# Layer 1 of a four-layer kernel with one weight product for scores, and the ternary test of layer 4's weights on ScalarE

## The chip, the cores and the metric

The kernel runs on one core of a Trainium2 chip. The metric is the device time of one execution in microseconds. The kernel before took 1845.1 us, the median of three runs (1843.9 to 1847.02).

## The reference

Four layers in a row, each `x = x + layernorm(layer(layernorm(x)))`, on x of 4 batches x 1024 tokens x 256 features in float32:

- Layer 1, attention with one head: `q = x Wq`, `k = x Wk`, `v = x Wv`, causal scores `q k^T / 16`, softmax, times v.
- Layer 2: `sqrt((x cos(theta + theta_noise))^2 + (x sin(phi + phi_noise))^2)`, two 256x256 products.
- Layer 3, causal attention with 16 heads of 16 features, and a product with `w_o`.
- Layer 4, a feed-forward net with ternary weights (-1, 0 or 1) and a scale per output: two products 256 to 1024 (SiLU of one times the other), two products 1024 to 1024 with GELU, one back to 256.

## The kernel before

The five engines each get a list of units in a common order, made by `order_first` to `order_fourth`; semaphores join them, and between layers all five meet at a barrier. Products are of split numbers: every operand is a high part (rounded to TensorE's fast float32 type) and a low part (the rest), and `mm3` (L567) makes three products of them: high x high, high x low, low x high. The high part is copied by ScalarE from PSUM, then VectorE subtracts it for the low part (`low`, L1179).

**Layer 1.** For each batch, x is normalised half a batch at a time (`stats1`, `apply1`), turned by TensorE (`tr1`) and split into `xT1`. `qk1(b, h, m, c)` projects a half batch of 512 tokens to queries (m = 0) or keys (m = 1), 128 output features at a time: 6 products of 512 columns. `val1(b, t)` projects two token tiles to values: 12 products of 256 columns. Then come eight tiles of 128 queries. Tile i: `scores1` (6 or 12 products, up to 512 columns each, over the tokens up to the diagonal), VectorE's row maximum (`mx`), ScalarE's exponential (`exps1`), TensorE's transposes of the probabilities (`turn1`), their split on ScalarE and VectorE (`pT_hi`, `pT_lo`), and `weigh1`, the product with the values. The list goes: scores of tile i, turn of tile i-1, exponential of i, then some side work (`side[i]`: the next batch's `tr1`, `qk1`, `val1`, `stats1`, `apply1`), then `weigh1` of tile i-1. Batch 3 has no next batch to project. `xT1` has one buffer; queries, keys and values have two.

Each of the 32 tiles also has one slot for something else. The first nine compute cos and sin for layer 2 (`trig`, `waves`). The later 23 test layer 4's weights: layer 4 has a fast form that is exact only if its weights survive rounding to the fast type, so the kernel reads every weight piece (`PIECES`, 48 of 128 rows x up to 512 columns), rounds it on ScalarE (`rround`, L928) and counts on VectorE where the rounded piece differs (`rcompare`, L1309, which also sums into `changed`). After a comparison SyncE issues the next load into the same buffer (`rload`, L1712). The other 25 pieces are tested in layer 2. `verdict` sums `changed`, and the flag picks the form of layer 4.

**Layer 2.** Eight groups n of four token tiles: `tr2` and `trlo2` turn and split, `tile2` is 6 products of 512 columns, ScalarE squares (`sq`), VectorE adds the squares (`power2`, `pw`, L1349), after the fourth ScalarE takes the root (`root2`, L949). The result is normalised (`ostats2` on VectorE, `stat_out`; `oapply2` on ScalarE, `y` at L968), GpSimd adds it to x (`add2`, L1595). VectorE also normalises group n+2 (`stats2`, `apply2`, `xn` at L1176). VectorE's order within a group: output statistics, a comparison, squares, input statistics, low half, comparison, squares, low half, comparison, squares, four `xn`, comparison, squares.

Of the kernel before, what the change touches and what calls it, by code (L numbers as in the profile page):

```python
# [8 lines left out]
HID = 1024  # L9
# [18 lines left out]
i32 = mybir.dt.int32  # L28
RSQRT_GUESS = float(0x5F3759DF)
# [27 lines left out]
def plain(ap):  # L57

    return ap.bitcast(f32)
# [44 lines left out]

def order_first():

    out, outs, late, todo = [], [], [], []
# [10 lines left out]
    first = NT - TRIG_STEPS  # L118
    rnd = list(range(first))
    loads = list(range(first))  # L120
    for b in range(B):
        side = [[] for _ in range(ST)]
        if b + 1 < B:
            n = b + 1
            p = project(n)
            side = [[("tr1", n, 0, 0), ("tr1", n, 0, 1), ("stats1", n, 1), p[0]], [p[1], ("apply1", n, 1), p[2]],
                    [p[3], ("tr1", n, 1, 0), ("tr1", n, 1, 1)], [p[4], p[5]], [p[6], p[7]], [p[8], p[9]], [p[10]], [p[11]]]
# [6 lines left out]
        for i in range(ST):  # L134
# [29 lines left out]
    out += [("rcompare", n_) for n_ in late]  # L164
# [5 lines left out]
PIECES = [(name, c, o, min(PIECE, cols)) for name, chunks, cols in  # L170
          (("w1", KC, HID), ("w2", KC, HID), ("h1", HC, HID), ("h2", HC, HID), ("w3", HC, D))
          for c in range(chunks) for o in range(0, cols, PIECE)]
FIRST = NT - TRIG_STEPS


def order_second():

    out, outs, late, loads, todo = [], [], [], list(range(FIRST, len(PIECES))), list(range(FIRST, len(PIECES)))
    out += [("rload", loads.pop(0)) for _ in range(4)]

    def settle():
        for u in late:
            out.append(u)
            if u[0] == "rcompare" and loads:
                out.append(("rload", loads.pop(0)))
# [8 lines left out]

    def rnd():
        if todo:
            n = todo.pop(0)
            out.append(("rround", n))
            late.append(("rcompare", n))
# [5 lines left out]
    for n in range(2 * B):  # L205
        for t in range(HALF):
# [13 lines left out]
            rnd()  # L220
    settle()
    out += outs + [("add2", 2 * B - 1)]
    while todo:
        rnd()
        settle()
# [105 lines left out]
def sandwich(nc, x_in, wq0, wk0, wv0, theta, phi, theta_n, phi_n, wqkvT, woT, w1T, w2T, h1T, h2T,  # L331
             w3T, s1, s2, sh1, sh2, s3, out):
    ctx = ExitStack()
    with ctx:
# [10 lines left out]
        hands_back = {"tr1": "dve", "qk1": "dve", "val1": "dve", "turn1": "dve", "weigh1": "act",  # L345
# [114 lines left out]
        with ExitStack() as ph:  # L460
            y1 = sb(ph, "y1", [P, 2, HALF, D])
            flat_y = y1[:, :, :, :].rearrange("p h t d -> p (h t d)")
            xT1 = [sb(ph, f"xT0_{k}", [P, KC, S], f32r) for k in ("hi", "lo")]
            qT = [[sb(ph, f"qT{i}_{k}", [P, KC, S], f32r) for k in ("hi", "lo")] for i in range(2)]
            kT = [[sb(ph, f"kT{i}_{k}", [P, KC, S], f32r) for k in ("hi", "lo")] for i in range(2)]
            v1 = [[sb(ph, f"v{i}_{k}", [P, ST, D], f32r) for k in ("hi", "lo")] for i in range(2)]
            raw1 = sb(ph, "raw", [P, 2, PIECE])
            raw_hi1 = sb(ph, "raw_hi", [P, 2, PIECE], f32r)
# [4 lines left out]
        spare1 = raw1[:, :, :].rearrange("p k (t d) -> p (k t) d", d=D)  # L473
        raw_w0 = [flat_y[:, n * KC * D:(n + 1) * KC * D].rearrange("p (c n) -> p c n", c=KC) for n in range(3)]
        angles = [raw1[:, 0, :], raw1[:, 1, :]]
        noise, turns = plain(raw_hi1[:, 0, :]), plain(raw_hi1[:, 1, :])

        with ExitStack() as ph:
# [5 lines left out]
            raw2 = sb(ph, "raw2", [P, 4, PIECE])  # L484
            raw_hi2 = sb(ph, "raw_hi2", [P, 4, PIECE], f32r)
# [78 lines left out]
        def tensor(e):  # L564
# [24 lines left out]
            def qk1(b, h, m, c):  # L589
                u = ("qk1", b, h, m, c)  # L590
                w.wait_ge(*done("dve", "weights1"))
                w.wait_ge(*back(ring1, u))
# [3 lines left out]
                    [((w0[m][0][:, k, c * P:(c + 1) * P], w0[m][1][:, k, c * P:(c + 1) * P]),  # L596
                      (xT1[0][:, k, cols], xT1[1][:, k, cols])) for k in range(KC)]).then_inc(*mark("pe", "qk1"))

            def val1(b, t):
                u = ("val1", b, t)  # L600
                bank = ring1.bank[u]
                w.wait_ge(*back(ring1, u))
                w.wait_ge(*done("dve", "tr1", b, 1, 1))
                for n in range(2):
                    tok = slice((t + n) * P, (t + n + 1) * P)
                    m = mm3(psum[:, bank, n * D:(n + 1) * D], [((xT1[0][:, k, tok], xT1[1][:, k, tok]),
# [35 lines left out]
            perform("first", {"tr1": tr1, "qk1": qk1, "val1": val1, "scores1": scores1, "turn1": turn1, "weigh1": weigh1,  # L642
# [212 lines left out]
        def scalar(e):  # L855
# [8 lines left out]
            def tr1(b, h, c):  # L864
                w.wait_ge(*done("pe", "tr1", b, h, c))
                if b:
                    w.wait_ge(*done("pe", "val1", b - 1, ST - 2))
                e.activation(xT1[0][:, c, h * BANK:(h + 1) * BANK], psum[:, ring1.bank["tr1", b, h, c], :],
                             ACT.Copy).then_inc(*mark("act", "tr1"))

            def qk1(b, h, m, c):
                w.wait_ge(*done("pe", "qk1", b, h, m, c))
                if b > 1:
                    w.wait_ge(*done("pe", "weigh1", b - 2, ST - 1))
                e.activation((qT, kT)[m][b % 2][0][:, c, h * BANK:(h + 1) * BANK], psum[:, ring1.bank["qk1", b, h, m, c], :],
# [48 lines left out]
            def rround(n, raw, hi, first, bufs, tag):  # L924
                k, cols = (n - first) % bufs, PIECES[n][-1]
                w.wait_ge(sem(f"rload{tag} {k}"), 16 * ((n - first) // bufs + 1))
                w.wait_ge(*nth("dve", "rcompare", n - bufs if n - first >= bufs else -1))
                e.activation(hi[:, k, 0:cols], raw[:, k, 0:cols], ACT.Copy).then_inc(*mark("act", "rround"))  # L928

            perform("first", {"weights1": weights1, "tr1": tr1, "qk1": qk1, "val1": val1, "exps1": exps1, "turn1": turn1,  # L930
                              "weigh1": weigh1, "waves": waves, "rround": lambda n: rround(n, raw1, raw_hi1, 0, 2, 1),
# [32 lines left out]
            def oapply2(n):  # L964
                rstd, term = moments["out"][3:]
                w.wait_ge(*done("dve", "ostats2", n))
                for t in range(HALF):
# [5 lines left out]
                               "rround": lambda n: rround(n, raw2, raw_hi2, FIRST, 4, 2),  # L973
# [164 lines left out]
        def vector(e):  # L1138
# [84 lines left out]
            def tr1(b, h, c):  # L1223
                w.wait_ge(*done("act", "tr1", b, h, c))
                cols = slice(h * BANK, (h + 1) * BANK)
                low("tr1", xT1[1][:, c, cols], psum[:, ring1.bank["tr1", b, h, c], :], xT1[0][:, c, cols])

            def qk1(b, h, m, c):
                w.wait_ge(*done("act", "qk1", b, h, m, c))
                cols, T = slice(h * BANK, (h + 1) * BANK), (qT, kT)[m][b % 2]  # L1230
                low("qk1", T[1][:, c, cols], psum[:, ring1.bank["qk1", b, h, m, c], :], T[0][:, c, cols])
# [73 lines left out]
            def rcompare(n, raw, hi, first, bufs):  # L1305
                k, cols = (n - first) % bufs, PIECES[n][-1]
# [51 lines left out]
            def verdict():  # L1358
                w.wait_ge(*done("dve", "rcompare", len(PIECES) - 1))
# [5 lines left out]
                               "power2": power2, "ostats2": ostats2, "rcompare": lambda n: rcompare(n, raw2, raw_hi2, FIRST, 4),  # L1365
# [320 lines left out]
        def sync(e):  # L1686
# [19 lines left out]
            def rload(n, raw, first, bufs, tag):  # L1706
                name, c, o, cols = PIECES[n]
                if tag == 1:
                    w.wait_ge(*done("dve", "waves"))
                if n - first >= bufs:  # L1710
                    w.wait_ge(*done("dve", "rcompare", n - bufs))
                e.dma_start(raw[:, (n - first) % bufs, 0:cols],  # L1712
                            weights[name][c * P:(c + 1) * P, o:o + cols]).then_inc(sem(f"rload{tag} {(n - first) % bufs}"), 16)

            def xloads(n):
                for k in range(n, 2 * B):
# [3 lines left out]
                              "rload": lambda n: rload(n, raw1, 0, 2, 1), "end": lambda: barrier(e, w, "first")})  # L1720
# [117 lines left out]
```

## Time and profile before

| | us |
|---|---|
| median of three runs | 1845.1 |
| the profiled execution | 1851.76 |
| its span | 1850.0 |
| TensorE busy | 1601.2 (87%) |
| VectorE busy | 1010.3 (55%) |
| ScalarE busy | 831.3 (45%) |
| GpSimd busy | 425.9 (23%) |
| mean granted TensorE clock | 0.894 |

PE is TensorE, PEld its weight loads, DVE VectorE, ACT ScalarE, POOL GpSimd, SP SyncE; SPq is SyncE's DMA issue. Layer 1 fills the first 278.3 us of the span and layer 2 the next 120.8. A row of a timeline gives start, duration, engine, line, operation, output and input, count, and in brackets how long the engine sat idle and what ended that. TensorE's products overlap: the distance of two starts, not the duration, tells what one costs.

### The profile page before, as it was taken

To read this page: it belongs to the slowest core of one execution; us is meant where nothing else is said; L and a number is where in the kernel's file an instruction comes from. 1 tells how busy PE (TensorE), PEld (TensorE's weight loads), DVE (VectorE), ACT (ScalarE), POOL (GpSimd) and SP (SyncE) were. 2 spreads that over 40 slices of the span, in tenths; PEclk is the share of its full clock that TensorE was granted. 3 is DMA by queue.
4 is the path that set the end of the run, shared out by engine and by line. 5 is a ranking of instruction groups with operands and counts; after the bars stand their busy time and mean duration, and the time that the engine had idled before them with its cause. 6 is when DMAs were issued, how large, how long until landed. Compare 5 with 4: busy or idle time off the path is not lost.

```text
span 1850.0 us, 24362 instructions
## 1 busy us (share of the span) xinstructions
PE 1601.2 (87%) x8658; PEld 1130.1 (61%) x8658; DVE 1010.3 (55%) x2889; ACT 831.3 (45%) x1686; POOL 425.9 (23%) x927
## 2 busy tenths in 40 slices
PE   6988856625799999998999995599999999999996
PEld 5877754524345445444545333488888888888885
DVE  5867547843766777767686832223334343333432
ACT  3454425631246565655565662234334353433432
POOL 2222221140233256235414323100101001010101
PEclk9999987867569799979998877699999999999998
DMA  3011102225603540741263100900000000000000
GB/s 120 12 35 35 46 17 89 88 80 74 86 1 47 82 71 13 96 59 44 42 87 59 36 2 23 289 12 0 23 1 23 1 24 1 23 23 1 12 1 23
DMA packets 52930, 83.34 MB, mean 45 GB/s; under 512 B 6784, under 2 KB 41216, under 8 KB 49920
## 3 DMA queue, kind: packets, MB, share of 16 engines
q1 hardware_dynamic: 46512, 68.85, 18.9%
q0 software_dynamic: 5712, 12.06, 2.1%
q10 hardware_dynamic: 576, 0.79, 0.4%
q8 instruction: 70, 1.15, 0.3%
q14 instruction: 60, 0.49, 0.1%
HBM read 43.40 MB, written 12.58 MB: 30 GB/s over the span
## 4 chain that ended last, share of the span: by engine, by line
PE 68%; DVE 16%; ACT 5%; issue 4%; POOL 2%; DMA 2%; SPq 1%; POOLq 1%; ACTq 0%; DVEq 0%
PE psum L831 25%; PE psum L571 13%; PE psum L746 7%; PE psum L805 6%; PE psum L731 6%; PE psum L712 4%; PE psum L844 3%; DVE mxs L1412 3%; PE psum L575 3%; DVE masked L1418 3%; ACT pr L1036 2%; DVE stat_out L1145 1%; DVE stat_in L1145 1%; SPq L1753 1%; DVE raw L1309 1%
## 5 line engine op out<-in xcount | busy, mean ns | idle before, releaser
L831 PE MATMUL psum<-fh_hi,fWh 128*128 128x512 f32 x1024 | 399.0, 390 | 0.0
L831 PE MATMUL psum<-fh_lo,fWh 128*128 128x512 f32 x1024 | 398.4, 389 | 0.0
L1036 ACT ACTIVATE pr<-psum 128x512 f32<-128x512 f32 (+3 forms) x768 | 321.8, 493 | 136.6 <-PE psum L731 131.4
L1181 DVE TENSOR_TENSOR fh_lo<-fraw,fh_hi 128x512 fp32r<-128x512 f32 x192 | 132.9, 692 | 380.0 <-ACT fh_hi L1100 335.3
L1418 DVE CUSTOM_DVE_ANT_0 masked<-psum,later 128x128 bf16<-128x128 f32 (+3 forms) x512 | 220.8, 487 | 96.8 <-PE psum L712 95.3
L731 PE MATMUL psum<-Qs,Ks 50*128 50x512 f32 (+3 forms) x768 | 234.1, 423 | 20.9 <-ACT pr L1036 12.3
L1096 ACT ACTIVATE fraw<-psum,fsch 128x512 f32<-128x512 f32 x128 | 86.5, 676 | 301.6 <-PE psum L831 301.6
L712 PE MATMUL psum<-Ks,Qs 48*128 48x512 f32 (+3 forms) x768 | 181.9, 466 | 40.3 <-DVE mxs L1418 18.0
L831 PEld LDWEIGHTS psum<-fh_lo,fWh 128*128 128x128 f32 x1024 | 192.3, 188 | 39.7
L831 PEld LDWEIGHTS psum<-fh_hi,fWh 128*128 128x128 f32 x1024 | 192.2, 188 | 39.7
L746 PE MATMUL psum<-pr,va 128*32 128x512 f32 (+3 forms) x1536 | 188.1, 566 | 0.0
L731 PEld LDWEIGHTS psum<-Qs,Ks 50*128 50x128 f32 x768 | 120.8, 209 | 107.0 <-ACT pr L1036 69.6
L712 PEld LDWEIGHTS psum<-Ks,Qs 48*128 48x128 f32 x768 | 84.3, 212 | 153.2 <-issue 59.1
L1412 DVE TENSOR_REDUCE mxs<-psum 128x2 f32<-128x1024 f32 x128 | 149.9, 1216 | 38.1 <-PE psum L712 37.9
L1580 POOL TENSOR_TENSOR term_in<-rstd_in 128x4 f32<-128x4 f32 x66 | 14.5, 220 | 518.4 <-DVE rstd_in L1162 515.0
L1649 POOL TENSOR_SCALAR_AFFINE_SELECT pr<-pr 128x512 f32<-128x512 f32 x128 | 81.9, 641 | 130.4 <-ACT pr L1036 130.0
L805 PE MATMUL psum<-fxT_hi,fWw 128*128 128x512 f32 x256 | 101.4, 396 | 10.7 <-DMA fWw<-in_w1T 10.2
L805 PE MATMUL psum<-fxT_lo,fWw 128*128 128x512 f32 x256 | 100.9, 394 | 0.0
L1100 ACT ACTIVATE fh_hi<-fraw 128x512 fp32r<-128x512 f32 x128 | 80.9, 632 | 4.0
L1580 POOL TENSOR_TENSOR term_out<-rstd_out 128x4 f32<-128x4 f32 x78 | 17.4, 223 | 274.0 <-DVE rstd_out L1162 269.9
L1595 POOL TENSOR_TENSOR x<-x,y 128x1024 f32<-128x1024 f32 x16 | 40.5, 2529 | 132.0 <-ACT y L968 97.8
L571 PE MATMUL psum<-v_hi,pT_hi 128*128 128x256 f32 x144 | 46.3, 321 | 25.5 <-DVE pT_lo L1181 25.3
(228 smaller groups left out, 2807.6 us busy)
## 6 DMA issues: line engine op xcount, KB each, us to landing
Qs<-q_hi SPq DMA_DIRECT2D x60, 128.0 KB, 5.4
Ks<-k_hi SPq DMA_DIRECT2D x60, 128.0 KB, 5.0
xr<-x_stream SPq DMA_DIRECT2D x9, 512.0 KB, 4.4
x<-in_x SPq DMA_DIRECT2D x8, 512.0 KB, 8.0
raw<-in_h1T SPq DMA_DIRECT2D x16, 256.0 KB, 2.6
raw<-in_h2T SPq DMA_DIRECT2D x16, 256.0 KB, 2.8
x_stream<-x SPq DMA_DIRECT2D x8, 512.0 KB, 3.2
shared_xn<-x_stream SPq DMA_DIRECT2D x8, 512.0 KB, 5.6
```

What stands on the lines that cost most here:

```text
L571: m = e.matmul(o, l, r, start=start and n == 0, stop=stop and n == len(ops) - 1)
L712: e.matmul(psum[:, pairs3.bank[u] + side, 0:width], Qs[g % NST][r, pair, i * P:(i + 1) * P], Ks[g % NST][r, pair, k0:k0 + width], start=Tr ...
L731: e.matmul(psum[:, ring3.bank[u], 0:width], Ks[g % NST][r, pair, j * P:(j + 1) * P], Qs[g % NST][r, pair, q0:q0 + width], start=True, stop ...
L746: m = e.matmul(psum[32 * ct:32 * ct + VB, 7, BANK - width:BANK], va[b % 2][:, j, head * VW:head * VW + VB], pr[:, 2 * (s % 3) + pair, side ...
L805: m = e.matmul(psum[:, bank, :], f.W[name][:, c, cols], xT[:, n % 2, c, :], start=(c, k) == (0, 0), stop=(c, k) == last)
L831: m = e.matmul(psum[:, ring4.bank[u], :], f.W[name][:, c, oc * P:(oc + 1) * P], h[:, c, :], start=(c, k) == (0, 0), stop=(c, k) == last)
L1036: e.activation(pr[:, 2 * (s % 3) + pair, side, 0:width], psum[:, ring3.bank["st3", s, pair, side], 0:width], ACT.Exp, scale=SC1).then_inc( ...
L1096: e.activation(f.raw[:, k, :], psum[:, bank, :], ACT.Gelu, scale=f.sc[("h1", "h2")[layer]][:, oc:oc + 1]).then_inc(*mark("act", "dense4"))
L1181: return e.tensor_tensor(dst, src, plain(hi), ALU.subtract).then_inc(*mark("dve", kind))
L1412: m = e.tensor_reduce(mxs[:, g % 2, k0 // BANK, :, pair, i], psum[:, bank:bank + 2, 0:width], AX.X, ALU.max)
L1418: m = e.tensor_tensor_reduce(masked[:, 2 * pair + side, 0:width], psum[:, bank + side, 0:width], later[:, BANK - width:], 1.0, LEAST, ALU. ...
L1649: e.affine_select(out=blocks, in_=blocks, compare_op=ALU.is_ge, fill=0.0, base=0, pattern=[[0, 2], [0, 2], [1, P]], channel_multiplier=-1) ...
```

## The change

In layer 1 the queries' and keys' weights are multiplied with each other: `fold1` makes `Wq Wk^T` (2 units of 6 products of 256 columns), split into `wm`. One projection `qk1(b, h, c)` with `wm` takes the place of queries and keys, and the scores are formed against `xT1`, which now has two buffers. So 4 units of `qk1` per batch go, with their copies and subtractions. `Wq` and `Wk` are laid out transposed. The units stand in another order: in batch 0 a value unit first, then the fold, the other values, then the queries; for the later batches one query unit in each of tiles 0, 1, 4 and 5, and one value unit in each of tiles 3, 5, 6 and 7.

The weight test reads pieces of 128 x 1024 numbers (22 in all, each 512 KB, two buffers). `weighed` is one ScalarE activation over the low 16 bits of every number, taken as unsigned integers, that sums them into `changed`; rounding to the fast type can only matter where they aren't zero. It overwrites the piece. The comparison on VectorE is gone. All 22 stand in layer 1, one in each tile's slot from tile 1 of batch 1 on; layer 2 has none.

```diff
+PIECES = [(name, c, n) for name, chunks, n in (("w1", KC, 1), ("w2", KC, 1), ("h1", HC, 1), ("h2", HC, 1), ("w3", HC, HC // 2))
+          for c in range(0, chunks, n)]
...
     def project(b):
-        return ([("qk1", b, half, m, c) for half in range(2) for m in range(2) for c in range(KC)]
-                + [("val1", b, t) for t in range(0, ST, 2)])
+        return ([("val1", b, t) for t in range(0, ST, 2)] + [("qk1", b, half, c) for half in range(2) for c in range(KC)])
-    out += project(0) + [("apply1", 1, 0)]
+    vals = project(0)[:ST // 2]
+    out += vals[:1] + [("fold1", 0), ("fold1", 1)] + vals[1:] + project(0)[ST // 2:] + [("apply1", 1, 0)]
...
-            side = [[("tr1", n, 0, 0), ("tr1", n, 0, 1), ("stats1", n, 1), p[0]], [p[1], ("apply1", n, 1), p[2]],
-                    [p[3], ("tr1", n, 1, 0), ("tr1", n, 1, 1)], [p[4], p[5]], [p[6], p[7]], [p[8], p[9]], [p[10]], [p[11]]]
+            side = [[("tr1", n, 0, 0), ("tr1", n, 0, 1), ("stats1", n, 1), p[4]], [p[5], ("apply1", n, 1)],
+                    [("tr1", n, 1, 0), ("tr1", n, 1, 1)], [p[0]], [p[6]], [p[1], p[7]], [p[2]], [p[3]]]
...
-                for n_ in late:
-                    out.append(("rcompare", n_))
+                if rnd:
+                    out.append(("weighed", rnd.pop(0)))
                     if loads:
                         out.append(("rload", loads.pop(0)))
-                late = [rnd.pop(0)]
-                out.append(("rround", late[0]))
...
+            def fold1(c):
+                u = ("fold1", c)
                 w.wait_ge(*done("dve", "weights1"))
+                w.wait_ge(*back(ring1, u))
+                mm3(psum[:, ring1.bank[u], 0:D],
+                    [((w0[0][0][:, k, c * P:(c + 1) * P], w0[0][1][:, k, c * P:(c + 1) * P]), (w0[1][0][:, k, :], w0[1][1][:, k, :]))
+                     for k in range(KC)]).then_inc(*mark("pe", "fold1"))
+            def qk1(b, h, c):
+                u, X = ("qk1", b, h, c), xT1[b % 2]
+                w.wait_ge(*done("dve", "fold1", 1))
...
             def scores1(b, i):
-                n, Q, K = b * ST + i, qT[b % 2], kT[b % 2]
+                n, Q, K = b * ST + i, qT[b % 2], xT1[b % 2]
...
+                w.wait_ge(*done("dve", "qk1", b, 1, 1))
...
+            def weighed(n):
+                piece = pieces1[n % 2]
+                w.wait_ge(sem(f"rload {n % 2}"), 16 * (n // 2 + 1))
+                e.activation(piece, piece.bitcast(u16).rearrange("p (n k) -> p n k", k=2)[:, :, 0], ACT.Copy,
+                             accum_out=changed[:, n:n + 1]).then_inc(*mark("act", "weighed"))
...
-            def rcompare(n, raw, hi, first, bufs):
-                k, cols = (n - first) % bufs, PIECES[n][-1]
-                w.wait_ge(*done("act", "rround", n))
-                r = raw[:, k, 0:cols]
-                e.scalar_tensor_tensor(r, r, 1.0, plain(hi[:, k, 0:cols]), ALU.mult, ALU.not_equal,
-                                       accum_out=changed[:, n:n + 1]).then_inc(*mark("dve", "rcompare"))
...
+            def rload(n):
+                name, c, chunks = PIECES[n]
+                w.wait_ge(*done("dve", "waves"))
+                if n > 1:
+                    w.wait_ge(*done("act", "weighed", n - 2))
+                e.dma_start(pieces1[n % 2].rearrange("p (c n) -> p c n", c=chunks),
+                            rows(weights[name])[:, c:c + chunks, :]).then_inc(sem(f"rload {n % 2}"), 16)
...
-        "x": a["L0_attn_x"], "wq0": a["L0_attn_Wq"], "wk0": a["L0_attn_Wk"], "wv0": a["L0_attn_Wv"],
+        "x": a["L0_attn_x"], "wq0": a["L0_attn_Wq"].T, "wk0": a["L0_attn_Wk"].T, "wv0": a["L0_attn_Wv"],
```

## Rows read from the trace of the kernel before

**Rows 1.** By stretch: its length; PE, PEld, DVE, ACT, POOL busy; clock; DMA share

```profile
0.00:38.70 38.70, 22.90 (x118) 19.86 (x118) 22.39 (x63) 12.52 (x20) 9.77 (x48) 1.00 0.45 143
38.70:208.40 169.70, 154.56 (x982) 134.63 (x982) 123.89 (x354) 81.67 (x174) 41.10 (x125) 0.97 0.09 28
208.40:278.30 69.90, 42.85 (x249) 37.48 (x246) 34.32 (x117) 21.60 (x48) 19.14 (x51) 0.82 0.09 28
278.30:399.10 120.80, 69.56 (x258) 52.43 (x258) 90.08 (x292) 65.71 (x130) 19.53 (x8) 0.75 0.27 85
399.10:1850.00 1450.90, 1311.37 (x7056) 885.72 (x7056) 739.61 (x2065) 649.78 (x1315) 336.38 (x695) 0.90 0.23 42
```

**Rows 2.** Chain of waits in layer 1 (start, duration, what)

```profile
62.92 6.31 PE psum L571 x36
...
168.28 0.60 DVE kT_lo L1181
168.88 0.61 DVE raw L1309 x2
```

**Rows 3.** Timeline of the opening, TensorE's products and one VectorE pair

```profile
17.95 0.78 PE L571 MATMUL psum<-xT_hi,w_hi 128*128 128x512 f32 x1
...
19.37 0.63 PE L571 MATMUL psum<-xT_hi,w_hi 128*128 128x512 f32 x1
19.58 1.28 DVE L1181 TENSOR_TENSOR xT_lo<-psum,xT_hi 128x512 fp32r<-128x512 f32 x2
19.80 0.63 PE L571 MATMUL psum<-xT_lo,w_hi 128*128 128x512 f32 x1
...
24.88 0.39 PE L571 MATMUL psum<-xT_hi,w_lo 128*128 128x512 f32 x1
25.11 0.39 PE L571 MATMUL psum<-xT_hi,w_hi 128*128 128x512 f32 x1
...
31.03 0.28 PE L571 MATMUL psum<-w_hi,xT_hi 128*128 128x256 f32 x1
31.15 0.28 PE L571 MATMUL psum<-w_lo,xT_hi 128*128 128x256 f32 x1
```

**Rows 4.** First test of a piece; 512 KB loads; a 1024-column activation

```profile
107.36 10.32 SPq L1712 DMA_DIRECT2D raw<-in_w1T  x3
109.99 0.64 ACT L928 ACTIVATE raw_hi<-raw 128x512 fp32r<-128x512 f32 x1
...
xr<-x_stream SPq DMA_DIRECT2D x9, 512.0 KB, 4.4
x<-in_x SPq DMA_DIRECT2D x8, 512.0 KB, 8.0
...
L949 ACT ACTIVATE y<-pw 128x1024 f32<-128x1024 f32 x8 | 8.5, 1058 | 22.8 <-DVE pw L1349 22.8
```

**Rows 5.** Chain of waits in layer 2, the start of two groups

```profile
311.03 1.41 DVE stat_out L1145 x4
...
325.23 1.08 DVE stat_out L1145 x3
```

**Rows 6.** Timeline of layer 2 about GpSimd's add, in two groups

```profile
317.70 2.07 ACT L968 ACTIVATE y<-y,term_out,rstd_out 128x256 f32<-128x256 f32 x4
319.74 3.43 DVE L1176 TENSOR_SCALAR xn<-x,mv_in,rstd_in 128x256 f32<-128x256 f32 x4
319.84 2.53 POOL L1595 TENSOR_TENSOR x<-x,y 128x1024 f32<-128x1024 f32 x1 [11.69 <-ACT y L968]
323.31 1.09 PE L575 MATMUL psum<-ident,xn 128*128 128x128 f32 x4 [1.40 <-DVE xn L1176]
323.70 0.41 DVE L1349 TENSOR_TENSOR pw<-sq 128x256 f32<-128x256 f32 x1
...
372.68 2.39 POOL L1595 TENSOR_TENSOR x<-x,y 128x1024 f32<-128x1024 f32 x1 [8.73 <-ACT y L968]
373.12 2.24 DVE L1349 TENSOR_TENSOR pw<-sq 128x256 f32<-128x256 f32 x1 [1.58 <-ACT sq L943]
```

More of the change, by code:

```diff
@@ L28 @@
 i32 = mybir.dt.int32
+u16 = mybir.dt.uint16
 RSQRT_GUESS = float(0x5F3759DF)
@@ L102 @@
     ("val", "val1 val3")) for kind in kinds.split()}
+PIECES = [(name, c, n) for name, chunks, n in (("w1", KC, 1), ("w2", KC, 1), ("h1", HC, 1), ("h2", HC, 1), ("w3", HC, HC // 2))
+          for c in range(0, chunks, n)]
 def order_first():
-    out, outs, late, todo = [], [], [], []
+    out, outs = [], []
     pre = [[("stats1", b, h) for h in range(2)] for b in range(B)]
@@ L112, in project @@
     def project(b):
-        return ([("qk1", b, half, m, c) for half in range(2) for m in range(2) for c in range(KC)]
-                + [("val1", b, t) for t in range(0, ST, 2)])
-    out += project(0) + [("apply1", 1, 0)]
+        return ([("val1", b, t) for t in range(0, ST, 2)] + [("qk1", b, half, c) for half in range(2) for c in range(KC)])
+    vals = project(0)[:ST // 2]
+    out += vals[:1] + [("fold1", 0), ("fold1", 1)] + vals[1:] + project(0)[ST // 2:] + [("apply1", 1, 0)]
     trig = [u for n in range(2) for u in (("trigload", n), *[("trig", n, k) for k in range(3)])] + [("waves",)]
-    first = NT - TRIG_STEPS
-    rnd = list(range(first))
-    loads = list(range(first))
+    rnd = list(range(len(PIECES)))
+    loads = list(range(len(PIECES)))
     for b in range(B):
@@ L167, in order_first @@
     return out + [u for u in outs if u] + [("end",)]
[L170 to L173, printed above, removed]
 def order_second():
-    out, outs, late, loads, todo = [], [], [], list(range(FIRST, len(PIECES))), list(range(FIRST, len(PIECES)))
-    out += [("rload", loads.pop(0)) for _ in range(4)]
+    out, outs, late = [], [], []
     def settle():
@@ L193, in tr @@
         late.append(("trlo2", n, c))
[L195 to L199, printed above, removed]
     tr(0, 0)
@@ L595, in qk1 @@
                 mm3(psum[:, ring1.bank[u], :],
-                    [((w0[m][0][:, k, c * P:(c + 1) * P], w0[m][1][:, k, c * P:(c + 1) * P]),
-                      (xT1[0][:, k, cols], xT1[1][:, k, cols])) for k in range(KC)]).then_inc(*mark("pe", "qk1"))
+                    [((wm[0][:, k, c * P:(c + 1) * P], wm[1][:, k, c * P:(c + 1) * P]),
+                      (X[0][:, k, cols], X[1][:, k, cols])) for k in range(KC)]).then_inc(*mark("pe", "qk1"))
             def val1(b, t):
-                u = ("val1", b, t)
+                u, X = ("val1", b, t), xT1[b % 2]
                 bank = ring1.bank[u]
+                w.wait_ge(*done("dve", "weights1"))
                 w.wait_ge(*back(ring1, u))
@@ L1225, in tr1, with fold1, qk1 @@
                 cols = slice(h * BANK, (h + 1) * BANK)
[L1226 to L1231, printed above, removed]
+                low("tr1", xT1[b % 2][1][:, c, cols], psum[:, ring1.bank["tr1", b, h, c], :], xT1[b % 2][0][:, c, cols])
+            def fold1(c):
+                w.wait_ge(*done("act", "fold1", c))
+                low("fold1", wm[1][:, c, :], psum[:, ring1.bank["fold1", c], 0:D], wm[0][:, c, :])
+            def qk1(b, h, c):
+                w.wait_ge(*done("act", "qk1", b, h, c))
+                cols, T = slice(h * BANK, (h + 1) * BANK), qT[b % 2]
+                low("qk1", T[1][:, c, cols], psum[:, ring1.bank["qk1", b, h, c], :], T[0][:, c, cols])
             def val1(b, t):
@@ L1358, in verdict @@
             def verdict():
-                w.wait_ge(*done("dve", "rcompare", len(PIECES) - 1))
+                w.wait_ge(*done("act", "weighed", len(PIECES) - 1))
                 e.tensor_reduce(cnt[:, :], changed[:, :], AX.X, ALU.add).then_inc(*mark("dve", "verdict"))
@@ L1719, in sync @@
             perform("first", {"weights1": weights1, "xload": xloads, "trigload": trigload,
-                              "rload": lambda n: rload(n, raw1, 0, 2, 1), "end": lambda: barrier(e, w, "first")})
+                              "rload": rload, "end": lambda: barrier(e, w, "first")})
             def add2(n):
```

74 lines of the change are left out of this document (25 added, 49 removed).

## The prediction

> **What bounds the kernel now.** The table by stretch comes first [rows 1]. Layer 1 takes the first 278.3 us: an opening of 38.7 (first halves loaded and normalised, batch 0 projected), batches 0 to 2 in 169.7, batch 3 in 69.9. Layer 2 ends at 399.1; layers 3 and 4 take the other 1450.9, and the diff leaves their code alone. In batches 0 to 2 TensorE is busy 154.6 of 169.7 us at a granted clock of 0.97. In batch 3, which has no next batch to project, it is busy 42.9 of 69.9. In layer 2 VectorE is busy 90.1 of 120.8 and TensorE 69.6.
>
> Next comes the chain of waits [rows 2]. In the tiles where a projection stands beside large score products it is TensorE alone: 36 products in 6.31 us. In the small tiles it is VectorE, and there both things that the change takes away stand in it: the low half of a key (0.60) and the comparison of a weight piece (0.61), each just ahead of the row maximum that lets the next exponential start. In layer 2 the chain is VectorE nearly throughout: one group of four tiles, from one start of `stat_out` to the next, takes 14.20 us [rows 5] and holds four comparisons.
>
> The profiled execution took 1851.76 us for its span of 1850.0. The median of the three timed runs is 1845.1, 6.7 less. I work out differences in the trace and take them from the median.
>
> **Layer 1, opening.** Before: 48 products of 512 columns and 48 of 256. At full clock they start 0.23 and 0.12 us apart, in the first 3.4 us 0.43 apart [rows 3]: 8 x 0.43 + 40 x 0.232 + 48 x 0.12 = 18.5. After: 24 of 512 and, with the fold's 12, 60 of 256. With 3.4 us at the low level for the first 16, this is 3.4 + 44 x 0.12 + 24 x 0.232 = 14.3, so 4.2 less. But the first unit is now a value projection, and that waits for the last low half of x^T, which VectorE ends at 19.58 + 1.28 = 20.86; the first query projection started at 17.95 [rows 3]. That gives 2.9 back: -1.3. The fold's eviction (two copies, two subtractions of 256 columns) lies beside 36 value products of 0.12, 4.3 us: nothing. Without that cover it would cost about 2.
>
> **Batches 0 to 2.** Each loses 24 products of 512 columns (24 x 0.232 = 5.6 us of TensorE), four copies on ScalarE and four subtractions on VectorE. Not all of it can be had, since the new lists leave tile 2 with transposes alone and tile 3 with one value unit. Once the next scores are done, the way to the weighted sum is maximum, reciprocal, low half of the turned probabilities: about 1.3 us at tile 2, 1.6 at tile 3, 1.9 at tile 4 (0.35 for the small instructions, the rest grows with the tile). I went tile by tile and took at each the later of TensorE's list and VectorE's list.
> - Batch 2. Tile 1: the comparison ahead of the maximum goes (0.6), then a key's low half and another comparison (1.2) [rows 2]. Tile 2: again one of each, 1.3. Tile 4: six products fewer, 1.4. Tiles 5 to 7 keep their length, because a query unit (6 x 0.232) takes the place of a value unit (12 x 0.12). Together 4.5.
> - Batch 0. VectorE computes the angles there and there are no comparisons: 0.6 at each of tiles 1 and 2, 1.4 at tile 4. Together 2.6.
> - Batch 1. 0.6 at tile 1, 1.3 at tile 2, 1.4 at tile 4, 0.5 at tile 7, less the wait below: 3.8 - 1.3 = 2.5.
>
> **The test on ScalarE.** A 128x1024 activation took 1.06 us [rows 4]; with reading the accumulator I take 1.25, against 0.64 for the old rounding of 512 columns. No row shows one that reads every other 16-bit word; from below it is 1.06, from above twice that. It stands behind the eviction of the weighted sum and ahead of the copy of the turned probabilities. From tile 3 on the next scores (1.4 us and more) cover it, and at tile 1 VectorE's statistics do. At tile 0 of batches 2 and 3 the scores are 128 columns wide and nothing does: 0.5 each, so batch 1 comes to -2.0 and batch 2 to -4.0. At 2.1 us each the test would stand out in about half of the 22 tiles by 0.8, some 9 us: that end is kept for the range.
> The test also has a new wait: its piece is 512 KB. The first load is issued at 107.36 as before, and the old test began at 109.99 [rows 4]. A 512 KB load landed in 4.4 us, which is 111.8. ScalarE stands still until then, and behind it wait the copy of the turned probabilities, the next exponential and the evictions: 1.8 us late, plus the longer test, less what TensorE has to do meanwhile; I take 1.3, once. Later pieces are loaded two tiles ahead (9 us in the small tiles), so at 4.4 they are there.
>
> **Batch 3.** Only comparisons go. Two stood ahead of a maximum, one ahead of the last low half (0.6 each) [rows 2]; the others ran under TensorE: -1.9. Layer 1 in all: 1.3 + 2.6 + 2.0 + 4.0 + 1.9 = 11.8.
>
> **Layer 2.** 25 comparisons go (17 of 512 columns at 0.61 [rows 2], 8 of 256 at 0.34, an estimate from it: 13.1 us of VectorE), with 25 copies on ScalarE and their loads. What is late next? After four additions of squares the group needs GpSimd's add, and while this runs VectorE stands: of four normalisations started at 319.74 two passed, and the four ended only 0.8 after the add of 319.84 to 322.37; an addition of squares, 0.41 by itself, took 2.24 under the add of 372.68 [rows 6]. Laid out anew from the start of `stat_out`, with each instruction's duration as in this group: statistics 2.4, squares 0.34, input statistics to 5.1, two low halves and two squares to 7.0. ScalarE, after the input's root, a copy and a square, ends its four `y` (2.07) at 7.7 and the add runs from 7.75 to 10.2. The normalisations mostly pass ahead of it, but the last squares end 0.3 to 0.7 after the add; with root (1.06) the next group starts at 11.6 to 12.1. Mean 11.85: 2.35 less in each of three groups, 1.5 and 1.3 in the two with three and four pieces of 256 columns (each piece 0.27 shorter from the start), 1.1 in the first, where TensorE is late next: 11.0. TensorE at its low level needs 24 x 0.43 [rows 3] + 2 x 1.09 [rows 6] = 12.5 for a group; its clock was 0.75 here [rows 1], so I take 0.8 off: -10.2. The bounds are -7, if always at the low level, and -13.1, all that is removed.
> The Trainium skill has the reason for this limit (GPSIMD Engine Reference, Specifications): GpSimd shares its SBUF interfaces with VectorE and contends with VectorE's instructions that have two SBUF inputs. The trace agrees by that 2.24 against 0.41 [rows 6]. Were it not so, the group would be near 10 us and layer 2 some 19 shorter.
>
> Sum: 11.8 + 10.2 = 22.0, and 1845.1 - 22.0 gives **1823**.
>
> **Rivals.**
> A. All of it is had: the tiles stay bound by TensorE (72 x 0.232 = 16.7), opening 1.3, comparisons in layer 1 2.9, layer 2 13.1: 34.0, 1811. For it: 91% busy in batches 0 to 2. Against it: kT_lo and the comparison stand in the chain, so TensorE already waited there, and the add holds layer 2.
> B. ScalarE holds the tiles: the test is nearer 2 us or its loads land late (of eight loads of this size issued together in the opening the median landed in 8.0 [rows 4]), 0.6 in each of 22 tiles: 22 - 13 = 9, 1836. Against it: ScalarE was busy 81.7 of 169.7 [rows 1].
> C. **Slower.** TensorE's clock in batches 0 to 2. With gaps at tiles 2 and 3 it may be granted less than 0.97. Its work at full clock is 154.6 x 0.97 - 16.7 = 133.3, beside 15 us of idle: at 0.75, the clock of layer 2, 133.3 / 0.75 + 15 = 192.7, 23 more than now. Opening, batch 3 and a layer 2 at its low bound give 10 back: 1858. It decides below 0.81 (133.3 / 0.81 + 15 = 179.6, 10 more). For it: batch 3 had just 0.82 at 61% busy, and layers 3 and 4 had 0.90 at 90% [rows 1]. Against it: the new share is about 46 of 54 us, near the present one, and gaps stay under 3 us.
> D. The low halves don't come out as zero and layer 4 takes its other branch: hundreds of us. Weights of -1, 0 and 1 have empty low halves: 0.01.
>
> **Chances.** Forecast 0.62, A 0.13, B 0.18, C 0.06, D 0.01. The range 1810 to 1836 reaches from A to B. A measurement of this kernel tells 0.2%, 3.7 us, from no change. Faster 0.91 (forecast, A, nearly all of B), same 0.03, slower 0.06.
>
> **What would show it.** Opening: first product of batch 0 near 20.9, first scores near 37.4. Batches 0 to 2 in about 161 us with TensorE still at 0.95 or more and idle 16 to 19; one ScalarE wait of about 2 us for `raw` at the first test and none later; tests of 1.06 to 1.1 us. Layer 2's groups at 11.6 to 12.4, with the squares held to the add's end. Layers 3 and 4 within 2 us of 1451. The forecast is wrong if the tests make ScalarE the releaser of the small tiles, if the clock falls, or if the groups of layer 2 stay above 13.

## The result, and the profile after

The changed kernel took 1822.8 us (median of four runs, 1816.4 to 1824.1) against 1844.5 for the kernel before (four runs, 1839.7 to 1847.0): a ratio of 0.988, 95% interval 0.985 to 0.991, or 21.7 us less. The forecast was 1823.0. Its profiled execution took 1824.12 us for a span of 1822.4, at a clock of 0.898. Executions over 1.5% longer than the fastest of their kernel, all at a low clock, are left out of the medians and ratios below.

The table by stretch, first of the kernel before with batches 0 to 3 apart, then of the changed kernel. The cuts stand where a batch's first scores are complete (the small product with `tri` behind them), and "first scores at" means that mark throughout. Columns as in [rows 1]; the clock is the mean of the stretch, and a "low stretch" is one of some 4 us in which it falls to 0.50 or near it.

```profile
38.70:91.70 53.00, 48.67 (x307) 42.32 (x306) 41.44 (x112) 22.43 (x49) 10.89 (x37) 0.97 0.03 11
91.70:150.30 58.60, 52.75 (x339) 46.05 (x338) 43.03 (x128) 31.36 (x66) 16.59 (x50) 0.97 0.11 32
150.30:208.10 57.80, 52.84 (x339) 45.97 (x339) 39.35 (x115) 27.57 (x62) 13.61 (x38) 0.97 0.12 39
208.10:278.30 70.20, 43.15 (x252) 37.78 (x250) 34.39 (x117) 21.90 (x49) 19.14 (x51) 0.82 0.09 29
```

```profile
0.00:38.40 38.40, 19.78 (x106) 17.71 (x106) 20.48 (x61) 10.89 (x18) 9.77 (x48) 1.00 0.44 144
38.40:90.20 51.80, 45.48 (x283) 39.59 (x283) 39.27 (x108) 20.51 (x45) 10.90 (x37) 0.90 0.04 11
90.20:145.60 55.40, 49.00 (x314) 43.77 (x312) 37.47 (x113) 32.77 (x68) 15.21 (x50) 0.91 0.23 76
145.60:197.10 51.50, 45.55 (x315) 40.27 (x315) 31.72 (x93) 29.66 (x66) 11.91 (x38) 1.00 0.25 83
197.10:263.30 66.20, 40.74 (x253) 36.04 (x251) 28.81 (x99) 25.38 (x56) 16.54 (x51) 0.89 0.16 48
263.30:371.00 107.70, 64.61 (x259) 48.40 (x259) 76.94 (x242) 54.33 (x105) 19.26 (x9) 0.80 0.13 44
371.00:1822.40 1451.40, 1310.02 (x7056) 884.16 (x7056) 739.22 (x2065) 650.00 (x1315) 336.53 (x695) 0.90 0.23 42
```

Both layers got shorter: layer 1 from 278.3 to 263.3, layer 2 from 120.8 [rows 1] to 107.7. Together that is 28.1 us, six more than forecast, and six more than the medians differ; layers 3 and 4 stand at 1451.4 against 1450.9. In batches 0 and 1 the clock was 0.90 and 0.91 instead of 0.97, in batch 2 it was 1.00.

In the opening, the first product and two pairs further on (timeline):

```profile
21.12 0.55 PE L550 MATMUL psum<-w_hi,xT_0hi 128*128 128x256 f32 x1 [2.71 <-DVE xT_0lo L1175]
...
25.31 0.41 PE L550 MATMUL psum<-w_lo,w_hi 128*128 128x256 f32 x1
25.52 0.41 PE L550 MATMUL psum<-w_hi,w_lo 128*128 128x256 f32 x1
...
26.32 0.28 PE L550 MATMUL psum<-w_hi,xT_0hi 128*128 128x256 f32 x1
26.44 0.28 PE L550 MATMUL psum<-w_lo,xT_0hi 128*128 128x256 f32 x1
```

The first unit waits for the low half of x^T, as worked out. But a distance of 0.21 from start to start, instead of the 0.12 of [rows 3], lasts to 26.2. That is 5.1 us instead of the 3.4 assumed, although the clock column says 1.00 here. I call this the half rate.

The test, as groups of ScalarE's instructions and its first start:

```profile
L922 ACT ACTIVATE raw<-raw 128x1024 f32<-128x1024 uint16 x22 | 23.1, 1052 | 1.1 <-DMA raw<-in_w1T 1.1
L922 ACT ACTIVATION_READ_ACCUMULATOR raw<-raw 128x1 f32 x22 | 4.2, 192 | 0.0
...
108.77 1.06 ACT L922 ACTIVATE raw<-raw 128x1024 f32<-128x1024 uint16 x1 [1.15 <-DMA raw<-in_w1T]
```

Each takes 1.05 us and 0.19 for the accumulator, the 1.25 assumed. There is one wait for a load, 1.15 us, and none later.

Layer 2 about GpSimd's add (timeline; the second line is the last of the first line's four), and the chain of waits of the same group:

```profile
299.08 3.42 DVE L1170 TENSOR_SCALAR xn<-x,mv_in,rstd_in 128x256 f32<-128x256 f32 x4
300.05 2.45 DVE L1170 TENSOR_SCALAR xn<-x,mv_in,rstd_in 128x256 f32<-128x256 f32 x1
299.89 2.46 POOL L1585 TENSOR_TENSOR x<-x,y 128x1024 f32<-128x1024 f32 x1 [9.30 <-ACT y L963]
302.42 0.41 DVE L1339 TENSOR_TENSOR pw<-sq 128x256 f32<-128x256 f32 x1
```

```profile
292.19 1.41 DVE stat_out L1139 x4
...
299.16 1.20 DVE xn L1170 x4
300.36 2.06 issue
...
303.96 1.08 DVE stat_out L1139 x3
```

The group lasts 303.96 - 292.19 = 11.77 us against the 14.20 of [rows 5]; 11.85 was forecast. The 2.06 of "issue" in the chain is the stall: three normalisations took 0.40 each, the fourth began 0.16 after the add and ended 0.15 after it (299.89 + 2.46 = 302.35), and the last squares, the root and the next group follow. But the same stall stood in the kernel before, where the second of the four was held, begun 0.22 after the add's start at 319.84 and ended 0.15 after its end (timeline):

```profile
320.06 2.46 DVE L1176 TENSOR_SCALAR xn<-x,mv_in,rstd_in 128x256 f32<-128x256 f32 x1
```

There the four took 3.43, here 3.42. So the group lost just its four comparisons, 14.20 - 4 x 0.61 = 11.76, and layer 2 lost the whole 13.1 us that VectorE was spared (busy 90.1 before, 76.9 after). By its length alone the group can't tell the forecast's account from the one by which all that is removed is had; the experiment with the short add, below, shows what the add is worth.

### The profile page after: what moved, and what is told of

It reads as the page before. It is cut to its first block, busy times and chain, and to the rows that moved or that the text cites. A ratio compares the mean times of both kernels' runs of the same rounds, so it can differ in the third digit from the quotient of the medians.

```text
span 1822.4 us, 24003 instructions
## 1 busy us (share of the span) xinstructions
PE 1575.2 (86%) x8574; PEld 1109.9 (61%) x8574; DVE 973.9 (53%) x2779; ACT 823.5 (45%) x1668; POOL 420.1 (23%) x927
## 3 DMA queue, kind: packets, MB, share of 16 engines
q8 instruction: 70, 1.15, 0.3%
## 4 chain that ended last, share of the span: by engine, by line
PE 69%; DVE 15%; ACT 5%; issue 5%; POOL 2%; DMA 2%; SPq 1%; POOLq 1%; ACTq 0%; DVEq 0%
PE psum L821 25%; PE psum L550 13%; PE psum L736 7%; PE psum L795 6%; PE psum L721 6%; PE psum L702 4%; PE psum L834 3%; DVE masked L1408 3%; PE psum L554 3%; DVE mxs L1402 3%; ACT pr L1030 2%; DVE stat_out L1139 1%; DVE stat_in L1139 1%; SPq L1742 1%; DVE mx L1242 1%
## 5 line engine op out<-in xcount | busy, mean ns | idle before, releaser
L702 PE MATMUL psum<-Ks,Qs 48*128 48x512 f32 (+3 forms) x768 | 180.1, 461 | 42.9 <-DVE mxs L1408 20.9
L554 PE MATMUL psum<-ident,shared_xn 128*128 128x128 f32 x128 | 23.8, 335 | 51.9 <-issue 19.2
L550 PE MATMUL psum<-v_hi,pT_hi 128*128 128x256 f32 x144 | 45.5, 316 | 25.8 <-DVE pT_lo L1175 25.7
```

The source lines that it names most:

```text
L550: m = e.matmul(o, l, r, start=start and n == 0, stop=stop and n == len(ops) - 1)
L702: e.matmul(psum[:, pairs3.bank[u] + side, 0:width], Qs[g % NST][r, pair, i * P:(i + 1) * P], Ks[g % NST][r, pair, k0:k0 + width], start=Tr ...
```

## The experiments

Every one has a trace. The ends of layers 1 and 2 repeat in them, while the whole does not: three profiled executions of the changed kernel reached layer 3 at 371.0, 371.3 and 369.5 us and then spent 1451.4, 1471.8 and 1444.4 us in layers 3 and 4. So the stretches carry the verdicts, and the medians stand beside them. The kernel before has one trace, so every gain by stretches counts from that one, and gains under 2 us are inside what the three traces differ by.

**The control.** The same code, run beside the next three.

> The changed kernel unaltered, as control and for a second trace. Theory (the gain is instructions removed, not clock): 20 to 23 us under the kernel before, 1.3 to 4 of it in each of batches 0 to 3, layer 2 at 107.7 us as in the first trace. Rival (part of what the first trace showed is the clock the execution happened to be granted): the clocks of batches 0 and 1 (0.90 and 0.91 in the first trace, 0.97 before) and of the last tile of batch 3 come out otherwise here, the ends of the batches move by 1 to 3 us with them, while the time of the whole stays within 3 us of 1822.8.

Layers 1 and 2 came out as in the first trace within 0.3 us, low stretches included; what differs is the last row:

```profile
90.20:145.70 55.50, 49.10 (x315) 43.88 (x315) 37.49 (x113) 32.88 (x68) 15.29 (x50) 0.91 0.22 76
...
371.30:1843.10 1471.80, 1331.78 (x7056) 894.58 (x7056) 740.51 (x2065) 650.63 (x1315) 337.58 (x695) 0.88 0.22 41
```

The median was 1821.4 (4 runs) against 1847.7 for the kernel before in the same set (13 runs), ratio 0.986 (0.979 to 0.994). The rival's clocks did not move here.

**The fold alone.** The diff's first part with the old test (copy, compare, pieces of 512 columns):

```
 weights' product, value units first, x^T as keys     as changed
-("weighed", n)
+("rround", n), ("rcompare", n)      # 23 pieces in layer 1, 25 in layer 2
```

> Only the first part of the change: folded weights, values first, x^T as keys; the old copy-and-compare test with pieces of 512 columns stays, in layers 1 and 2. Theory: the opening gives 0.3 to 1.3, batches 0 to 2 some 7 to 8 (0.6 to 1.4 at tiles 1, 2 and 4), batch 3 nothing, layer 2 stays at 120.8 with groups of 14.2: 7 to 9 us under the kernel before, near 1836. Rival (the thinner TensorE lists of tiles 2 and 3 leave the comparisons uncovered, or the clock falls): 5 us or less. Rival (TensorE's busy time is what counts): 17 us.

```profile
37.40:90.20 52.80, 46.65 (x282) 40.65 (x281) 39.31 (x108) 20.60 (x45) 10.90 (x37) 0.87 0.04 11
90.20:146.20 56.00, 48.45 (x314) 42.92 (x313) 40.79 (x124) 29.61 (x62) 16.55 (x50) 0.94 0.10 34
146.20:201.00 54.80, 47.38 (x315) 41.51 (x315) 37.02 (x112) 25.68 (x58) 13.60 (x38) 0.97 0.12 41
201.00:271.00 70.00, 42.90 (x252) 37.42 (x250) 34.29 (x117) 21.91 (x49) 19.16 (x51) 0.82 0.09 29
271.00:391.70 120.70, 69.38 (x258) 52.18 (x258) 90.13 (x292) 65.71 (x130) 19.53 (x8) 0.75 0.27 85
```

Layer 3 is reached 7.4 us earlier, inside the 7 to 9 expected: opening 1.3, batches 0.2, 2.6 and 3.0, batch 3 and layer 2 nothing. The batches' 5.8 is under the 7 to 8 expected for them: batch 0 gained just 0.2, at a clock of 0.87 instead of 0.97. The medians say 6.2 less (1841.5, 9 runs), but the ratio's interval, 0.996 (0.992 to 1.001), holds no change too.

**The test alone.** The diff's second part; queries and keys are projected apart as before.

```
-("fold1", c), ("qk1", b, half, c), keys = xT1[b % 2]
+("qk1", b, half, m, c),            keys = kT[b % 2]
```

> Only the second part: the test of the low halves by one activation on ScalarE, 22 pieces of 1024 columns, all in layer 1; queries and keys are projected apart as before. Theory: the comparisons' 0.6 us ahead of the maximum in batches 1 to 3 go (about 4 us), 1.3 to 2 come back in the wait for the first piece and the uncovered tests, and layer 2 gives 10 to 13: 12 to 15 us under the kernel before, near 1831, with layer 2 at 108 to 110. With the fold alone it adds up to the whole, 21.7, within 2. Rival (the ScalarE work in layer 1's tiles costs what VectorE is spared): layer 1 no shorter than 278 and 10 to 11 in all.

```profile
92.30:150.50 58.20, 52.42 (x339) 46.08 (x339) 39.78 (x117) 34.55 (x72) 15.27 (x50) 0.97 0.21 73
150.50:206.90 56.40, 52.40 (x338) 45.99 (x338) 34.11 (x97) 31.46 (x69) 11.92 (x38) 0.97 0.22 76
206.90:273.10 66.20, 40.65 (x251) 36.01 (x250) 28.80 (x99) 25.29 (x55) 16.55 (x51) 0.88 0.14 48
273.10:380.70 107.60, 63.55 (x259) 47.75 (x259) 76.96 (x242) 54.33 (x105) 19.29 (x9) 0.82 0.13 44
```

Layer 3 is reached at 380.7, 18.4 earlier: more than expected, 5.2 of it in layer 1 (the theory had 2 to 3) and 13.2 in layer 2. The medians say 18.0 less (1829.8, 4 runs; ratio 0.989, 0.982 to 0.996). With the fold's 7.4 that makes 25.8 of the whole's 28.1: the parts add up within 2.3.

**The add made short.** `add2` over one of a group's four tiles; three quarters of layer 2's addition to x are left out.

```
-add("add2", x[:, n * HALF:(n + 1) * HALF, :], y2[:, n % 2, :, :], ...)
+add("add2", x[:, n * HALF:n * HALF + 1, :], y2[:, n % 2, 0:1, :], ...)
```

> The changed kernel with GpSimd's addition of layer 2's result made over one of a group's four tiles; three quarters of that addition are left out. Theory (the add holds VectorE, and the group's 11.75 us come from it): the add takes about 0.65 instead of 2.46, the four normalisations 1.4 instead of 3.4, and the group falls to 10 to 10.5; layer 2 from 107.7 to 98 to 101. Rival (what ends the group is TensorE, or the sum of VectorE's own instructions): groups stay within 0.4 of 11.75.

```profile
297.02 1.80 DVE L1170 TENSOR_SCALAR xn<-x,mv_in,rstd_in 128x256 f32<-128x256 f32 x4
297.83 0.83 POOL L1585 TENSOR_TENSOR x<-x,y 128x256 f32<-128x256 f32 x1 [9.30 <-ACT y L963]
```

```profile
290.14 1.41 DVE stat_out L1139 x4
...
298.30 0.43 issue
...
300.28 1.41 DVE stat_out L1139 x4
```

The group fell to 10.14 us, the four normalisations from 3.42 to 1.80, the stall from 2.06 to 0.43, and layer 2 from 107.7 to 94.7, below the range expected. So the add's stall stands in the group in full: 1.63 us less of it is 1.63 us less group, and TensorE didn't hold it back.

**No test.** Its loads and activations are left out, the verdict set to zero; and **the test one tile later**, so that the first piece has landed.

```
-out.append(("weighed", rnd.pop(0)))            # no test; no ("rload", n) either
+if rnd and n > 9: out.append(("weighed", ...)) # later test, instead
```

> The changed kernel without the test of layer 4's weights: its loads and its 22 activations are left out, the verdict is set to zero. Theory: the wait for the first piece (1.15 us) and the tests that stand out at tile 0 of batches 1 to 3 go, the rest was covered: layer 1 shorter by 2 to 3 us, layer 2 as it is. Rival (ScalarE holds the small tiles): 6 us or more. Rival (the loads disturb other transfers or the test costs nothing): within 0.5.

> The changed kernel with every test one tile later, the first load issued where it was. Theory: the piece has landed when ScalarE comes to it, the wait of 1.15 us at the first test goes and no other comes: batch 1 shorter by about 1 us, the last test still inside batch 3. Rival (TensorE, at its low level from 104 to 112 us, was late there anyway): batch 1 the same within 0.3 us.

Batches 1 to 3 without the test, then batches 1 and 3 with it one tile later:

```profile
90.30:145.70 55.40, 49.01 (x314) 43.88 (x313) 37.51 (x113) 26.75 (x55) 15.30 (x50) 0.91 0.00 1
145.70:196.90 51.20, 45.46 (x314) 40.23 (x313) 31.73 (x93) 21.66 (x49) 11.96 (x38) 1.00 0.01 1
196.90:264.00 67.10, 41.83 (x252) 36.41 (x251) 28.91 (x99) 17.40 (x40) 16.62 (x51) 0.86 0.00 1
```

```profile
90.30:145.50 55.20, 48.29 (x314) 43.01 (x314) 37.40 (x113) 31.70 (x65) 15.31 (x50) 0.94 0.20 67
...
198.50:266.90 68.40, 42.22 (x253) 37.53 (x251) 28.80 (x99) 26.27 (x58) 16.62 (x51) 0.85 0.17 54
```

Without 27 us of tests (23.1 + 4.2) batches 1 and 2 together are 0.3 us shorter, batch 3 is 0.9 longer at a lower clock, and layer 1 ends 0.7 later. In layer 1 the test costs nothing that the traces show, its wait for the load included: with only that wait taken away batch 1 was 0.2 shorter. In both traces TensorE was in a low stretch at that tile. Where it was not, in the trace with the short add, the wait was 1.46 us, and from that tile's exponential to the next took 4.2 us, against 3.8 at the same tile of batch 2, where nothing waits: 0.4 at most. The second kernel's layer 1 ended 3.6 later, by its clock as far as the traces tell: the opening was 1.0 shorter, but batch 0 gave back 1.1 (0.87), batch 2 1.5 (0.97 instead of 1.00), batch 3 2.2 (0.85; it also holds one test more). Both theories failed; the rivals held.

**The fold made early.** In the changed kernel TensorE idles from 18.4 to 21.1 and before 13.1. Here the weights are multiplied ahead of the second half's normalisation, and the queries come first again:

```
-("apply1", 0, 0), ("apply1", 0, 1), ...
-out += vals[:1] + [("fold1", 0), ("fold1", 1)] + vals[1:] + <queries>
+("apply1", 0, 0), ("fold1", 0), ("fold1", 1), ("apply1", 0, 1), ...
+out += <queries> + <values>
```

> The whole change, but the product of the two weights is computed before the second half of batch 0 is normalised, and batch 0's query products come ahead of its value products as in the kernel before. Theory: TensorE has the fold done in its idle time before the transposes and starts batch 0's products at about 18 instead of 21.1, on the first half of x^T alone; first scores 2 to 3 us earlier than 38.4, the whole 2 to 3 us under the changed kernel (near 1820). Rival (VectorE, which must make the fold's two low halves first, normalises the second half of the batch later by 1 to 2 us, and TensorE then runs dry after the first half): first scores no more than 1 us earlier, the whole within 1 us.

```profile
11.35 0.55 PE L549 MATMUL psum<-w_hi 128*128 128x256 f32 x1 [11.35 <-DVE w_lo L1213]
...
18.30 0.40 PE L549 MATMUL psum<-xT_0hi,wm_lo 128*128 128x512 f32 x1
18.54 0.39 PE L549 MATMUL psum<-xT_0hi,wm_hi 128*128 128x512 f32 x1
```

Batch 0 starts at 17.76, at 0.23 to 0.31 per product of 512 columns from the first on, and the first scores come at 32.05 instead of 38.42: 6.4 us, twice the expectation. The early products themselves, from 11.35 on, were 0.21 apart. The median was 1815.4 (5 runs) beside the control's 1821.4 (ratio to the kernel before 0.981, 0.975 to 0.987). This expectation hadn't reckoned with the slow first products. To part the two causes:

> The early fold, but with batch 0's value products ahead of its query products as in the changed kernel. The early fold with the queries first had its first scores at 32.05 us against 38.4. Theory: of those 6.4 us, 3.4 are the earlier start on the first half of x^T and fall away here; 3.0 are the fold's 12 products taken out of the stretch and the products at full rate from the first on, since TensorE has multiplied at 11.4 us already, and stay: first product at 21, spaced 0.12 at once, first scores at 35 to 35.5. Rival (the slow rate comes with the first products after any pause): spaced 0.21 for some 3 us again, first scores near 37.5.

```profile
21.03 0.55 PE L549 MATMUL psum<-w_hi,xT_0hi 128*128 128x256 f32 x1 [3.53 <-DVE xT_0lo L1174]
21.38 0.41 PE L549 MATMUL psum<-w_lo,xT_0hi 128*128 128x256 f32 x1
...
22.00:26.00 4.00, 4.00 (x21) 4.00 (x20) 0.69 (x1) 0.60 (x1) 0.80 (x4) 0.50 0.01 2
```

With the values first and 3.5 us of idleness ahead of them the products are 0.21 apart again and the first scores come at 37.05: the rival held. Here the clock column does show it, as 0.50. An early fold by itself gives 0.4 to 1.4 against the changed kernel's 37.5 to 38.4; the other 5.0 (37.05 to 32.05) came from the order, by which batch 0 starts 3.3 us sooner and at full rate. The half rate lasted 5.6 us in this one trace, the longest of all, so up to an us of that split is its chance.

**Where the clock falls.** In the traces with the fold, a low stretch stood in batch 0 near 52 us, behind tile 2, which has transposes alone. So six products went from tile 1 to tile 2, on the changed kernel and on the early fold:

```
-[p[5], ("apply1", n, 1)], [("tr1", n, 1, 0), ("tr1", n, 1, 1)]
+[("apply1", n, 1)], [p[5], ("tr1", n, 1, 0), ("tr1", n, 1, 1)]
```

> The changed kernel with one query product group (six products of 512 columns) moved from tile 1 to tile 2 of each batch, where TensorE had transposes alone. In three traces with the fold TensorE's granted clock fell in batch 0 near 52 us, right behind that thin tile, and in batch 1 near 104; in the kernel before and in the one with the new test alone it did not. Theory (the thin tile 2 brings the fall): the low stretches at 52 and 104 us go, batches 0 and 1 shorter by 1 to 3 us each. Rival (the fall follows the whole share of work, not this tile): a low stretch of the same length stands somewhere in batches 0 and 1, and they are the same within 1 us.

> The early fold (queries first) with the same six products moved from tile 1 to tile 2. If the thin tile brings the fall of the clock: layer 1 ends at 252 to 255 us instead of 256.8, the whole 2 to 5 us under the early fold. If not: within 1 us of 256.8.

```profile
37.80:88.40 50.60, 44.45 (x281) 38.62 (x280) 39.09 (x108) 20.49 (x45) 10.92 (x37) 0.93 0.04 11
88.40:145.90 57.50, 49.30 (x314) 43.82 (x314) 37.30 (x113) 32.86 (x68) 15.35 (x50) 0.91 0.21 74
...
200.30:268.60 68.30, 43.01 (x252) 37.31 (x251) 29.05 (x99) 25.44 (x56) 16.57 (x51) 0.82 0.14 47
```

Batch 0 won 1.2 us and its fall at 52 went, but the one at 104 stayed, batches 1 and 2 became 2.1 and 2.9 longer and layer 1 ended 5.3 later. On the early fold, layer 1 ended at 257.6, between that kernel's own 256.8 and 258.5. The thin tile explains neither the clock nor the time; what does stays open. The two kernels' times, 1819.6 (one run) and 1808.2 (median of 5; ratio 0.979, 0.973 to 0.984), lie with those of the changed kernel and the early fold.

**The early fold beside the changed kernel.**

> The early fold once more, beside the changed kernel on the same chip. Theory: its opening and batches repeat (first scores at 32.1, layer 1 ends at 256.8), and the whole is 6 to 7 us under the changed kernel. Rival (layers 3 and 4 give it back through the clock): the traces repeat, but the whole is less than 3 us under.

> The changed kernel beside the early fold. Theory: first two layers as in the two traces before (layer 2 starts at 263.3 to 263.6, layer 3 at 371.0 to 371.3), 20 to 25 us under the kernel before. Rival (the low stretches of the clock fall elsewhere in each execution): these two marks move by more than 1 us.

Layer 3 was reached at 365.9 and 369.5 (364.4 and 371.0, 371.3 before): 5.4 us apart in the mean. The medians are 1810.9 (5 runs; ratio 0.976, 0.969 to 0.984) and 1817.6 (6 runs; 0.984, 0.978 to 0.990) against 1847.1. So the early fold is the fastest here in both sets, by its traces some 5 us; the intervals of the two ratios overlap. In the third trace of the changed kernel the slow stretches did fall elsewhere: its half rate ended at 24.5 instead of 26.2 (first scores at 37.5), batch 1 had 0.97 and took 53.8 instead of 55.4, and batch 2 had 0.97 and took 53.0 instead of 51.5.

## Why the prediction was right, and where by luck

The direction and the median were right, and most of the mechanisms. The sum, 22.0, is 6 us short of what layers 1 and 2 gave, 28.1 in the first pair of traces; that is as far from the forecast as from rival A's 34.0.

- **Opening**: forecast -1.3, got -0.3. The start (21.12 against 20.9) was right. The half rate was taken as 3.4 us and lasted 5.1; where it ended at 24.0 instead of 26.2 (the fold alone, first scores at 37.4), the 1.3 were there.
- **Batches 0 to 2**: forecast -8.6 at a clock of 0.95 or more, got -10.7 at 0.94; idle time was 158.7 - 140.0 = 18.7, inside the 16 to 19. Batch 0 gave 1.2 instead of 2.6, at 0.90 instead of 0.97. Batch 1 gave 3.2 instead of 2.0, batch 2 6.3 instead of 4.0. The term that failed is **the test's cost in them**: 1.3 for the wait at the first piece and 0.5 at tile 0 of batches 2 and 3 each, 2.3 in all. Taken out altogether, the test gave back 0.3. The wait was there, 1.15 us of the 2 expected, and next to nothing came of it. What else is off goes with the clock as far as the traces tell, and cancels: in the traces where batch 2 had 0.97, as before, it took 52.9 to 53.0, so 1.5 of its 6.3 came with the 1.00, while batch 0, at 0.93, took 50.6 (the shifted list) and 50.7 (values first), near the forecast's 50.4, but also 51.9 (the early fold again).
- **Batch 3**: forecast -1.9, got -4.0. The comparisons' 1.9 is right at an unchanged clock: with the new test and 0.82, this batch took 68.3 (the shifted list) against 70.2. The rest goes with the clock: in the traces the batch took 68.3 at 0.82, 68.4 at 0.85, 67.1 at 0.86, 66.0 to 66.4 at 0.88 and 0.89, 64.8 at 0.91, and with the old test 70.0 to 70.2 at 0.82. Why the clock was mostly higher with the new test isn't shown.
- **Layer 2**: forecast -10.2, got -13.1, the end of its range. The three middle groups gave 7.16 against 7.05 (add to add, 42.34 to 35.18 us), the next two 2.8 as forecast. The first (to its add) gave 2.5 where I had put 1.1, because TensorE should have been late next; the end gave 0.6 where I had nothing; and the 0.8 for the low clock was not due: TensorE kept up at 0.80. What failed is the thought that something would be held back. The add's stall was in the group before and after, at the same length, and moved up with the group, so all that was removed was had. (The recorded reading that two of the four passed ahead of the add at 319.84 is off by one: the second was the held one.) That the add holds VectorE is right: the short add gave 10.14 us a group, where I had written near 10. Yet layer 2 was then 26.1 shorter than before, not 19.
- **Layers 3 and 4**: within 0.5 us of 1450.9 in the trace. By the medians, less layer 3's start and the 1.7 us around the span, they took 1844.5 - 1.7 - 399.1 = 1443.7 before and 1822.8 - 1.7 - 371.0 = 1450.1 after, though their code is the same. That difference hid my shortfall. It is most likely the clock, though the record has none for the four runs before. An estimate from the runs that have one: over 80 executions of six kernels, with the clock of layers 3 and 4 worked out from each run's mean and the traces, their time falls by 11.3 us for each 0.01, with a scatter of 2.1, and at 0.90 lies between 1446.2 and 1449.4 in all. Whether the changed kernel's 0.1 to 1.4 us more there than the kernel before (1447.0) is real stays open.
- **The rivals.** A (all of it is had) was near in layer 2, where its 13.1 came, and wrong in the tiles, where it had 16.7 and 10.7 came. B (ScalarE holds the tiles) is refuted by the kernel without the test. C, the clock, came in part: batches 0 and 1 fell to 0.90, but the three batches together had 0.94, far from the 0.81 from which it decides. In the fold alone batch 0 fell to 0.87 and gave 0.2 instead of 2.6.

By the medians of the two later sets the changed kernel stands at -26.3 and -29.5. The traces put the first two layers at 28 to 30 less, so the gain is more likely 26 to 29 us than 22: the forecast's 1823.0 was met to 0.2 us with two errors of 6 us that cancelled.

## What to carry to other kernels

When an engine is relieved, look at what holds it besides its own work, and ask whether that stays where it is or moves up with the rest. Here GpSimd's add held VectorE before and after alike, so the whole 13.1 us removed was had, and the stall itself was worth another 1.6 us a group. Work put on an idle engine costs nothing while the engine that waits for it is late for another reason; one wait of 1.15 us in a trace was worth 0.4 at most. And when work is taken from the start of a kernel, look at where the heavy engine stands idle before it: moving the weights' product there and starting on half of the input was worth 5 us, a fifth of the whole change, for an edit of two lines.

## What the runs showed of the hardware

- The first products after an idle stretch went at half rate, 0.21 us for 256 columns instead of 0.12, for 2.9 us (the fold alone) to 5.6 us (values first), with a clock column of 1.00 in all openings but that last one. Where TensorE had been at work since 11.35 and paused for 0.6 us at most, batch 0's products went at full rate from the first on, in three traces. The Trainium skill says that an idle array starts at half its clock and that the same kernel shows more or fewer such products from run to run (TensorE: Matmul & The Clock Gate, The HAM clock gate). The traces agree: first scores at 37.5 and 38.4 with the same code.
- Under GpSimd's add VectorE's normalisations, with one input tile each, stopped too: 3.42 us for four beside an add of 2.46, 1.80 beside one of 0.83. The Trainium skill calls the shared ports exclusive and held for a whole instruction (SBUF — State Buffer, Terms). The traces agree: those begun before the add took 0.40 each (one in the kernel before, three in the changed one), and the first begun behind the add's start took 2.46 and 2.45 and ended 0.15 after the add.
- ScalarE took 1.05 us for 1024 16-bit words, every other one in memory, and 1.06 for 1024 packed 32-bit words [rows 4]. Reading the accumulator behind it took 0.19.
